# A graph network's second attention: source rows gathered once per group of edges instead of once per item, with ScalarE copying an item's rows out of the ring

## What is computed

```python
xl = x @ Wl + bl
xr = x @ Wr + br
e = edge_attr @ We
m = xl[src] + xr[dst] + e
m = jax.nn.leaky_relu(m, NEG_SLOPE)
logits = m @ att
mx = jax.ops.segment_max(logits, dst, num_segments=n)
ex = jnp.exp(logits - mx[dst])
den = jax.ops.segment_sum(ex, dst, num_segments=n)
alpha = ex / (den[dst] + 1e-16)
out = jax.ops.segment_sum(xl[src] * alpha[:, None], dst, num_segments=n)
return out + bias_out
```

## Time and profile before

| | |
|---|---|
| Median of 3 runs | 4297.43 us (4296.95 to 4298.02) |
| Profiled execution | 4296.55 us, span 4294.7 us, mean granted TensorE clock 0.808 |
| PE busy | 3433.3 us, 80% of the span |
| PEld busy | 2674.9 us, 62% |
| DVE busy | 2652.6 us, 62% |
| ACT busy | 1616.2 us, 38% |
| POOL busy | 2562.0 us, 60% |
| DMA | 349.78 MB, mean 81 GB/s |

### The profile page before, as it was taken

One profiled execution on the slowest core, in us unless ns is written; L12 is line 12 of the kernel. 1 busy time (PEld: TensorE's weight loads), 2 busy tenths in 40 slices (PEclk: granted clock), 3 DMA queues, 4 the chain that ended last, 5 costly groups with the idle time before them and its releaser, 6 DMA issues. The chain is left out here.

```text
span 4294.7 us, 91663 instructions
## 1 busy us (share of the span) xinstructions
PE 3433.3 (80%) x20700; PEld 2674.9 (62%) x20793; DVE 2652.6 (62%) x6184; ACT 1616.2 (38%) x3137; POOL 2562.0 (60%) x2650
## 2 busy tenths in 40 slices
PE   6999999977777775766656666666665999999996
PEld 3777777754555543555545555455554888888894
DVE  5888888875666664433344333443335888888885
ACT  3666666644555553111121111211114333333334
POOL 4555555536777766777757777577772444444430
PEclk7999999988999995555565655655557999999998
DMA  3333333322333322222222222222222333333330
GB/s 118 89 101 100 99 99 101 99 69 65 80 80 81 80 66 60 69 67 67 68 61 68 67 67 67 60 67 68 67 67 73 109 107 111 108 106 111 108 93 15
DMA packets 293250, 349.78 MB, mean 81 GB/s; under 512 B 63536, under 2 KB 236755, under 8 KB 292915
## 3 DMA queue, kind: packets, MB, share of 16 engines
q0 software_dynamic: 98528, 229.12, 19.7%
q1 hardware_dynamic: 140481, 92.05, 8.0%
q10 hardware_dynamic: 54162, 27.77, 2.2%
HBM read 332.61 MB, written 16.07 MB: 81 GB/s over the span
## 5 line engine op out<-in xcount | busy, mean ns | idle before, releaser
L988 POOL DMA_INDIRECT gath<-source_rows_narrow,gine_idx x1176 | 1145.3, 974 | 429.9 <-issue 357.8
L1036 DVE TENSOR_TENSOR vs<-psum,gath 128x512 f32<-128x512 f32 x366 | 253.1, 692 | 804.9 <-SPq L973 677.9
L1142 POOL DMA_INDIRECT gath<-source_rows,idx_all x416 | 430.6, 1035 | 508.1 <-DVE vs L1263 351.3
L1002 PE MATMUL psum<-gine_lin,ea 32*128 32x128 f32 x2928 | 285.9, 479 | 516.1 <-DVE vs L1036 487.0
L760 POOL DMA_INDIRECT gath<-source_rows,idx_all x488 | 465.2, 953 | 374.6 <-PE psum L807 259.6
L760 POOL DMA_INDIRECT gath<-source_rows_narrow,idx_all x488 | 464.6, 952 | 205.3 <-issue 137.2
L1002 PEld LDWEIGHTS psum<-gine_lin,ea 32*128 32x128 f32 x2928 | 182.1, 294 | 618.3 <-DVE vs L1036 554.8
L790 PE MATMUL psum<-lk,att_b 128*128 128x512 f32 x732 | 373.9, 617 | 112.5 <-DVE lk L885 111.8
L807 PEld LDWEIGHTS psum<-gath,pt 128*128 128x128 f32 x2928 | 365.4, 192 | 36.8 <-DVE zsum L918 1.8
L1011 PE MATMUL psum<-hot,pm 128*128 128x128 f32 x1488 | 372.3, 429 | 17.0 <-ACT pm L1066 16.1
L1066 ACT ACTIVATE pm<-vs 128x512 f32<-128x512 f32 x186 | 117.3, 630 | 690.9 <-DVE vs L1036 686.4
(11 more groups left out here) (242 smaller groups left out, 6131.9 us busy)
## 6 DMA issues: line engine op xcount, KB each, us to landing
rel<-rel_rows SPq DMA_DIRECT2D x244, 128.0 KB
ea<-in_edge_attr_tiles SPq DMA_DIRECT2D x416, 64.0 KB
ea<-in_edge_attr ACTq DMA_DIRECT2D x366, 64.0 KB
gath<-source_rows_narrow,gine_idx POOLq DMA_INDIRECT x1176, 2.5
gath<-source_rows,idx_all POOLq DMA_INDIRECT x904
rel<-quad_rel_rows SPq DMA_DIRECT2D x104, 128.0 KB
gath<-source_rows_narrow,idx_all POOLq DMA_INDIRECT x488
source_rows<-ACC SPq DMA_DIRECT2D x12, 512.0 KB, 2.9
```

The source lines that it names most:

```text
L988: pool.indirect_dma_start(out=ring[:, g % RING, j, :], out_offset=None, in_=table1, in_offset=bass.IndirectOffsetOnAxis(ap=gine_idx[:, g, ...
L1002: last = e.matmul(E[:, j, :], ea[rows, s, :], gine_lin[rows, layer, :], start=True, stop=True)
L1036: v.tensor_tensor(vs[:, s, :].rearrange("p (j d) -> p j d", j=SUBS), E, ring[:, bass.ds(slot, 1), :, :].rearrange("p a j d -> p (a j) d"), ...
L1142: pool.indirect_dma_start(out=gath[:, q % 4, j, :], out_offset=None, in_=table, in_offset=bass.IndirectOffsetOnAxis(ap=quad_idx[:, q, j:j ...
```

## The change

In the second attention (`by_group`, that is one head) POOL gathers each of the 98 groups once into the ring of eight slots, with the indices that the GINE layers use (`gine_idx`), and reports each landing through `rows_landed` after it has issued the group behind. From the ninth group on it first reads `group_end` and waits until ScalarE has copied the rows of the last item that used the slot. ScalarE gets a new operation per item (`take`, line 868 of the changed kernel): it reads group and slot of item i + 1 from `groups_blocks`, waits for the landing and until item i - 3 has been summed, and copies 128x512 floats from the ring's slot to one of four fixed places in the unused half of ACC. PE transposes and multiplies from there and waits for `rows_taken` in place of the gather. The first attention is as before. The semaphores of the ring are now shared with the GINE layers, so the counts that they and the edge network wait for start elsewhere.

```diff
@@ gat_edges
+            by_group = heads == 1
+            rows = ACC[:, NODE_BLOCKS * D:NODE_BLOCKS * D + 4 * GROUP_EDGES].rearrange("p (s j d) -> p s j d", s=4, j=SUBS) if by_group else gath
...
                 @block.gpsimd
                 def _(pool):
+                    def report(g):
+                        pool.wait_ge(gi_gath[g % RING], 16 * SUBS * (g // RING + 1))
+                        pool.nop().then_inc(rows_landed, 1)
+
+                    if by_group:
+                        pool.wait_ge(gine_idx_in, 16)
+                        for g in range(GROUPS):
+                            if g >= RING:
+                                end = pool.value_load(group_end[0:1, g - RING:g - RING + 1], min_val=1, max_val=ITEMS)
+                                pool.wait_ge(rows_taken, end)
+                                pool.nop().then_inc(slot_free, 1)
+                            for j in range(SUBS):
+                                pool.indirect_dma_start(
+                                    out=ring[:, g % RING, j, :], out_offset=None, in_=dram,
+                                    in_offset=bass.IndirectOffsetOnAxis(ap=gine_idx[:, g, j:j + 1], axis=0)).then_inc(gi_gath[g % RING], 16)
+                            if g >= 1:
+                                report(g - 1)
+                        report(GROUPS - 1)
+                        return
                     for i in range(ITEMS):
...
                 @block.tensor
...
-                        e.wait_ge(gathered[s4], 16 * SUBS * (turn4 + 1))
+                        if by_group:
+                            e.wait_ge(rows_taken, i + 1)
+                        else:
+                            e.wait_ge(gathered[s4], 16 * SUBS * (turn4 + 1))
...
-                                last = e.transpose(T[h][:, j * P:(j + 1) * P], gath[:, s4, j, h * D:(h + 1) * D], ident)
+                                last = e.transpose(T[h][:, j * P:(j + 1) * P], rows[:, s4, j, h * D:(h + 1) * D], ident)
...
-                                last = e.matmul(O[h], pt[:, h, j, :], gath[:, s4, j, h * D:(h + 1) * D],
+                                last = e.matmul(O[h], pt[:, h, j, :], rows[:, s4, j, h * D:(h + 1) * D],
...
                 @block.scalar
...
                             a.activation(vs[:, h, :], T[h], ACT.Copy).then_inc(g_copied, 1)
+                        if by_group and not (isinstance(i, int) and i == ITEMS - 1):
+                            take(i + 1, (s4 + 1) % 4)
...
+                    def take(i, s4):
+                        _, (g, slot) = nc.values_load_multi_w_load_instructions(
+                            groups_blocks[0:1, bass.ds(i, 1), 0:2], engines=(mybir.EngineType.Activation,),
+                            min_val=0, max_val=GROUPS - 1)
+                        slot = nc.s_assert_within(slot, 0, RING - 1)
+                        a.wait_ge(rows_landed, g + 1)
+                        if not isinstance(i, int) or i >= 4:
+                            a.wait_ge(o_ready, before_h + i - 3)
+                        a.activation(rows[:, s4, :, :], ring[:, bass.ds(slot, 1), :, :].rearrange("p a j d -> p (a j) d"),
+                                     ACT.Copy).then_inc(rows_taken, 1)
...
                     mask(0, 0, number * PAIRS)
+                    if by_group:
+                        take(0, 0)
                     walk(a, front, back, mid, layer=number)
@@ gine_edges
-                    return 16 * SUBS * (layer * -(-(GROUPS - slot) // RING) + round + 1)
+                    return 16 * SUBS * ((layer + 1) * -(-(GROUPS - slot) // RING) + round + 1)
@@ mlp_edges
-            gathered_before = [16 * SUBS * 2 * -(-(ITEMS - m) // 4) for m in range(4)]
+            gathered_before = [16 * SUBS * -(-(ITEMS - m) // 4) for m in range(4)]
```

More of the change, by code:

```diff
@@ L708, in build @@
         gathered = [sem(f"gathered{s}") for s in range(4)]
+        gi_gath = [sem(f"group_gathered{s}") for s in range(RING)]
+        rows_landed, rows_taken, slot_free = (sem(f"gat1_{k}") for k in ("rows_landed", "rows_taken", "slot_free"))
         gat_sems = [sem(f"gat_{k}") for k in (
@@ L928, in build @@
         gi_ea = [sem(f"gine_ea_in{s}") for s in range(2)]
-        gi_gath = [sem(f"gine_gathered{s}") for s in range(RING)]
         gi_landed, gi_free = sem("gine_landed"), sem("gine_free")
```

## The result

| | before | after |
|---|---|---|
| Median | 4297.73 us (4294.72 to 4299.32, 6 runs) | 4313.57 us (4311.55 to 4315.59, 6 runs) |
| Ratio, 95% interval | | 1.0037 [1.0027, 1.0048] |
| Profiled span | 4294.7 us | 4310.0 us |
| Edge loop of the second attention, first to last score product | 612.4 us | 628.9 us |
| Four items of it | 20.13 us | 20.7 us |

The change makes the kernel 0.37% slower: 15.8 us by the medians, 16.5 us in the loop. The lines moved: 760 is now 773, 772 is 798, 780 is 806, 790 is 816, 799 is 825, 820 is 846, 837 is 876, 844 is 883, 881 is 922, 885 is 926.

A forecast was written before the change was run, and what follows sets the result against it. A PE-DVE chain was taken to bound the edge loop; with the change a two-item loop through ScalarE gives four items 20.84 us, 21 us over 121 steps, so 4296.55 becomes 4317.6, forecast 4318, range 4296 to 4340.

The forecast's parts named there:

- rival A: ScalarE's copy and address work are hidden in its idle time, so the pace stays 5.03 us, 4297 us; chance 0.17.
- No engine is full, the loop is paced by a chain: Second attention's edge loop: a chain through PE and DVE sets 5.03 us per item, not POOL's gathers.
- rival D: PE's share falls from 0.79 to 0.76 and the granted clock drops, adding over 100 us; chance 0.02.
- The address work begins when the PSUM copy starts: ACT's sequencer doesn't run past a waiting instruction, so 1.36 us of address work begins when line 820 starts.
- The loop over two items through the shared bank: Exponents and key transposes share one PSUM bank, tying ScalarE's delay to PE: 10.28 us for two items against 10.07.
- There is slack behind the PSUM copy: The ScalarE loop hid under the PE-DVE chain; address work up to 0.87 us plus the 0.53 us copy would be free.
- 10.28: Predicted us for two items without the branch, summed around the loop through ScalarE and the shared bank; 10.07 before.
- address work: ScalarE's two-word register load and nine register instructions ahead of the copy of rows: 1.36 us, bounds 1.20 to 1.75.
- hops: Estimated delays between an instruction's end and its waiter in the two-item loop: 0.10 us for two; half would give -6 us.
- "10.56" for the pair with the branch: Pair whose line 772 is behind the loop's branch: line 772 leads line 780 by 1.36 us, not 1.08, giving 10.56 us.
- +2 for the two copies ahead of the first exponent: At the loop's start ScalarE makes two copies before the first exponent, costing some 2 us once.
- -2 for the rows that come earlier: Fewer gathers spare transposes' waits for late rows, part of 3.4 us beyond the steady pace; 2 us taken back.

The follow-up runs named there:

- own bank: Changed kernel with the transposed exponents in a PSUM bank of their own in the second attention: 4299.04 us, ratio 1.0005.
- copy moved ahead: Changed kernel with ScalarE's register load and copy of rows for item i + 1 moved ahead of item i's PSUM copy: 4294.33 us, ratio 0.9995.
- control with the own bank: Kernel before with the transposed exponents of the second attention in a PSUM bank of their own: 4296.45 us, ratio 0.9999.

## Why the prediction was right, and where a term was off

The forecast was 4318 us with a range of 4296 to 4340; 4313.6 was measured. The range took in no change at all (rival A at 4297), so that the time lies in it says little by itself. The mechanism held at each place where it could be looked at:

- **No engine is full, the loop is paced by a chain.** Right: with a quarter of the gathers left out the pace is the same. PE's share of the stage was 0.80 and not the 0.76 of rival D, at a granted clock of 1.00.
- **The address work begins when the PSUM copy starts, not while ACT waits for it.** Right: line 861's load starts at 1207.5 (its row stands in the last section), behind the PSUM copy's start at 1207.41, which had followed 0.52 us of idle waiting. Rival A fell on this. The time from copy to copy was to be over 0.87 us and was 1.42 to 1.50.
- **The loop over two items through the shared bank.** Right: cutting the bank (own bank) or the delay (copy moved ahead) each brings the time back.
- **There is slack behind the PSUM copy.** Right: the exponent may come 1.55 us behind it at no cost, by the runs, where it came 0.75 before; the prediction said 1.40. For that it took 4.92 us for an ordinary step, where the two of this pair take 4.96 in the mean. Its own sum, 10.28 us at 1.89, set against the 9.92 that this pair takes, gives 1.53.

Term by term, for the pair without the branch, from 1205.81 to 1216.22 us:

| term | predicted | measured |
|---|---|---|
| score product to PSUM copy | 1.60 | 1.60 |
| address work | 1.36 | 1.50 |
| copy of rows | 0.53 | 0.54 |
| exponent with its read and hops, to the transposes | 0.91 | 0.91 |
| transposes to the copy from the bank | 0.72 | 0.70 |
| copy from the bank, with hops | 0.70 | 0.71 |
| key transposes to line 806 (was 780) | 1.08 | 1.08 |
| line 806 to DVE's add | 1.31 | 1.20 |
| add to leaky ReLU | 1.32 | 1.42 |
| leaky ReLU to score product | 0.75 | 0.75 |
| sum | 10.28 | 10.41 |

The 1.31 was read where DVE itself was late with its own row of work; waiting for PE it follows in 1.20 us.

The pair took 0.13 us more than predicted, by the address work above all, and the pair with the branch 0.23 us less: the errors run against each other, and that the sum of both came within 0.1 us is in part luck.

**The term that was most mis-sized is "10.56" for the pair with the branch.** The prediction added the full lateness of line 780 there, 0.28 us. Measured, from 1195.48 to 1205.81, the pair takes 10.33 us, and line 806 comes 1.09 us behind line 798 (1201.30 to 1202.39), as it does without a branch. So PE's sequencer was done with the branch while PE waited for the bank, and the lateness went under that wait. The step behind the branch is 5.3 to 5.4 us on PE, about as long as before (5.33); most of what the change costs is in the step two further on, 5.36 us where it was 4.97. Four items are 20.74 us where 20.84 was predicted, and 20.7 over the middle of the loop. The lengthening is 0.56 us over four items, 0.14 for each, and 17 us over 121 steps, where 0.177 and 21 us were predicted. That accounts for the 4 us by which the forecast was high.

**The ends of the loop.** 17 us from the pace and 16.5 measured leave -0.5; 0 was predicted, from +2 for the two copies ahead of the first exponent and -2 for the rows that come earlier. The +2 isn't shown. The first two steps take 13.7 us where they took 11.2, and 11.1 with the copy moved ahead; but they take 13.4 in the control with the own bank, which has no copy of rows. Between 998 and 1001 us the granted clock is 1.00 in the kernel before and with the moved copy, and 0.50 in the changed kernel and in that control, so the clock is in these 2.5 us too. The -2 can be read. In the last step of the kernel before the key transposes wait for a landing:

```profile
1594.69 0.42 PEld L772 LDWEIGHTS psum<-consts,gath 128*128 128x128 f32 x4 [1.11 <-DMA gath<-source_rows_narrow,idx_all]
```

That step takes 5.35 us and the fifth to the ninth together 26.8. With the copy moved ahead they take 4.84 and 25.4, with three gathers of four 4.84 and 25.5, in the control with unchanged gathers 5.25 and 26.2. So late rows cost the kernel before some 1.8 us in its profiled execution. With +2.5 and -1.8 some -1.2 us of the -0.5 stay unplaced.

**Beyond the loop** nothing changes that a run can show. In the profiled pair the loop starts 4.0 us later and the GINE layers take 4.9 us less (1565.0 us from the first to the last product of line 1042, 1569.9 before). The eight experiments lie between 1563.0 and 1567.1 us there, so it is the profiled execution of the kernel before that stands apart. The medians, which differ by 15.8 us, agree with the loop.

The page "DMA: Bandwidth & Descriptors" of the Trainium skill, section "Latency and other measured facts", gives a register load a floor of some 600 ns. The runs disagree: 491 ns for two words and 269 for one on ACT, 288 for one on POOL. With 600 for 491 the address work would be, as an estimate by that page, 1.53 to 1.61 us, where 1.42 to 1.50 was measured.

## What to carry to other kernels

Ask of added work first which instruction it stands ahead of, and how much slack the loops through that instruction have: the same work of 2.0 us per item cost 16 us over the loop behind the PSUM copy and nothing ahead of it. A dynamic address costs its engine 1.4 us of sequencer time, more than twice the copy it was for; put it behind an instruction that doesn't wait. And an engine that issues at a steady pitch isn't the pacer for that: look at what it waits for itself, or leave a part of its work out.

## What the runs showed of the hardware that was not expected

- **ACT's sequencer runs past an operation whose engine is still busy, and not past one whose semaphore is open.** With the copy moved ahead, line 853 stands ahead of the address work. It starts at 1201.21, when line 883 is nearly through, but the load of line 861, which comes behind it, starts at 1200.9 already (the first row below), and the copy of rows follows line 853 by 1.01 us, less than the 1.42 that the address work takes. In the changed kernel the load stands behind line 846, for which ACT waits 0.52 us, and starts only at 1207.5 (the second row, of the changed kernel). "Advanced Engine Details and Errata" of the Trainium skill, section "Sequencer Loop", has the sequencer push an engine instruction into a queue and lets the engine instruction wait for its semaphore. It doesn't say whether the sequencer goes on to the next one meanwhile. The traces show that it does for line 853, and that it doesn't for line 846, where the load comes only after the semaphore.

```profile
L861 ACTq TENSOR_LOAD <-groups_blocks x1: 491/491/491, 1200.9 to 1200.9; - x1
L861 ACTq TENSOR_LOAD <-groups_blocks x1: 492/492/492, 1207.5 to 1207.5; - x1
```

- **A second load of one word cost 0.61 us and not its own 0.27**, since two register operations and an assert come with it (69, 152 and 18 ns), and time passes between any two.
- **A sequencer's lateness behind a branch can be hidden.** (No run takes the branch away; it is read from the pattern of four steps.) The step behind the branch was 0.36 to 0.46 us longer than the others as long as PE was waited for; where PE waits for the bank, the long step without a branch is as long as it is, 5.36 us each.
